# Attention with the values as the stationary operand, output by column, sums by a matrix of ones

## The reference, cut to what matters

```python
q = norm(x) @ Wq.T (+ b_q)           # 16 heads of 16 columns
k, v = ctx @ Wk.T (+ b_k), ctx @ Wv.T (+ b_v)
probs = softmax(q @ k.T / 4)         # over the 77 keys, per head
out = (probs @ v) by heads           # 256 rows x 256 columns
x = x + tanh(g_xattn) * (out @ Wo.T + b_o)
```

## Time and profile before

| | |
|---|---|
| median of 3 runs | 866.01 us |
| profiled execution | 865.35 us, span 863.6 us |
| TensorE busy | 835.3 us (97%) |
| VectorE busy | 539.7 us (62%) |
| ScalarE busy | 427.2 us (49%) |
| attention of layer 0 | about 9 to 145 us |
| attention of layer 1 | about 242 to 382 us |

### The profile page before, as it was taken

How to read it: one execution, slowest core, us unless ns; L and a number is a source line. 1 busy time by engine, 2 the same in 40 slices (tenths; PEclk the granted TensorE clock), 3 DMA queues, 4 the chain that set the end, 5 groups by cost and what they waited for, 6 DMA issues and landing times.

```text
span 863.6 us, 17182 instructions
## 1 busy us (share of the span) xinstructions
PE 835.3 (97%) x5664; PEld 766.5 (89%) x5664; DVE 539.7 (62%) x1132; ACT 427.2 (49%) x938; POOL 276.7 (32%) x329
## 2 busy tenths in 40 slices
PE   8899999999979999999999999999999999999997
PEld 6788988999958989878887999999899999989986
DVE  4777764556687888465446574736456473645558
ACT  3666665777765666532323553616254361615331
POOL 5243414877773452145550001020200102020140
PEclk9999999999999999999999999999999999999999
DMA  5423237877520000201113432314233232413262
GB/s 209 116 69 128 66 117 286 260 219 224 175 77 8 7 6 6 87 17 44 60 44 90 133 90 70 106 41 134 60 97 95 80 89 61 128 39 100 64 194 99
DMA packets 74853, 86.26 MB, mean 100 GB/s; under 512 B 31418, under 2 KB 47484, under 8 KB 74678
## 3 DMA queue, kind: packets, MB, share of 16 engines
q1 hardware_dynamic: 67590, 69.65, 27.0%
q10 hardware_dynamic: 3664, 9.46, 3.1%
q0 software_dynamic: 3552, 6.55, 2.3%
HBM read 63.32 MB, written 23.63 MB: 101 GB/s over the span
## 4 chain that ended last, share of the span: by engine, by line
PE 83%; SPq 5%; DVE 4%; DMA 2%; ACT 2%; issue 2%; POOL 2%; DVEq 0%; ACTq 0%; POOLq 0%
PE score L292 13%; PE score L293 13%; PE score L294 13%; PE bank_p L298 11%; PE bank L603 7%; PE bank_p L299 6%; SPq L371 5%; PE bank_p L594 3%; PE bank L615 3%; PE bank L623 2%; PE bank L544 2%; PE score L583 2%; DMA v_blk<-values 1%; DVE residual L1911 1%; PE bank L957 1%
## 5 line engine op out<-in xcount | busy, mean ns | idle before, releaser
L1257 ACT ACTIVATE silu<-score 128x366 f32<-128x366 f32 (+1 forms) x144 | 72.6, 504 | 274.0 <-PE score L294 274.0
L298 PE MATMUL bank_p<-w_both,hid_hi 128*122 128x512 f32 (+1 forms) x432 | 152.5, 396 | 0.5 <-DVE hid_lo L1653 0.5
L1645 DVE TENSOR_TENSOR prod<-silu,score 128x366 f32<-128x366 f32 (+1 forms) x144 | 82.2, 571 | 110.6 <-ACT silu L1257 109.6
L292 PE MATMUL score<-xe_hi,w_both 128*128 128x366 f32 x448 | 147.4, 329 | 0.0
L293 PE MATMUL score<-xe_lo,w_both 128*128 128x366 f32 x448 | 147.3, 329 | 0.0
L294 PE MATMUL score<-xe_hi,w_both 128*128 128x366 f32 x448 | 147.2, 328 | 0.0
L2165 POOL DMA_INDIRECT slots_out<-yh,home_of x42 | 40.8, 972 | 331.0 <-DVE yh L1802 331.0
L299 PE MATMUL bank_p<-w_both,hid_lo 128*122 128x256 f32 (+1 forms) x432 | 120.8, 280 | 0.0
L298 PEld LDWEIGHTS bank_p<-w_both,hid_hi 128*122 128x122 f32 (+1 forms) x432 | 79.4, 184 | 21.5 <-DVE hid_lo L1653 1.6
L1981 POOL TENSOR_TENSOR w_both<-raw,w_both 128x512 fp32r<-128x512 f32 x62 | 83.4, 1374 | 24.6 <-ACT w_both L1037 17.8
L603 PE MATMUL bank<-v_blk,prob_t 128*128 128x136 f32 x640 | 83.9, 288 | 6.6 <-DMA v_blk<-values 6.2
(11 more groups left out here) (234 smaller groups left out, 1637.5 us busy)
## 6 DMA issues: line engine op xcount, KB each, us to landing
raw<-w_second_d SPq DMA_DIRECT2D x108, 256.0 KB, 2.7
raw<-w_first_d SPq DMA_DIRECT2D x56, 256.0 KB, 3.5
yh<-slot_rows SPq DMA_DIRECT2D x7, 674.6 KB
v_blk<-values SPq DMA_DIRECT2D x256, 5.0 KB, 2.0
slot_rows<-yh ACTq DMA_DIRECT2D x5, 771.0 KB, 3.3
slots_out<-yh ACTq DMA_DIRECT2D x5, 512.0 KB, 4.3
slot_rows<-yh SPq DMA_DIRECT2D x3, 771.0 KB, 5.7
raw<-w_first_d ACTq DMA_DIRECT2D x8, 256.0 KB, 3.8
```

Of the source, the lines that this page charges most:

```text
L292: nc.tensor.matmul(o, a_hi, b_hi, start=start, stop=False)
L298: nc.tensor.matmul(o, a_hi, b.rearrange("p c d -> p (c d)"), start=start, stop=False)
L1257: nc.scalar.activation(silu[0:rows_n, buf, 0:width], src, ACT.Silu).then_inc(silu_done, 1)
L1645: nc.vector.tensor_tensor(prod[0:rows_n, buf, 0:width], silu[0:rows_n, buf, 0:width], up, ALU.mult).then_inc(gu_free, 1)
```

## The change

The values become the stationary operand: for two heads 64 keys x 2 = 128 rows by 32 columns (`v_main`), and for the last 13 keys of the eight heads one full block (`v_rest`). The moving operand is `prob_t`, 256 queries wide. The output has head and dimension on partitions and queries along the row, so it needs no transposition. The sums come from the same matmuls with a matrix of ones. They stand 16 times over (128 partitions x 256), and `normalise_out` takes the reciprocal of all. The probabilities are laid out by head pairs: four transpositions, and for the 13 keys that are left four matmuls with the identity, each 32 columns of the array wide. The value bias goes by one product with Wo into layer 1's output bias. The value loads are 12 DMAs for each batch, into two alternating buffers. The order in the steps is moved accordingly.

```diff
-VW = P + HT
+PAIR = HG * HD                  # 32
+MAIN = P // HG                  # 64 keys
+REST = KV - MAIN                # 13 keys
+PW = KC - P + (-(KC - P)) % 32 + P      # 160
-        prob = [sb(f"prob{u}", [P, PT * P]) for u in range(4)]
-        v_blk = sb("v_blk", [P, KT * PT, VW])
+        prob = [sb(f"prob{u}", [P, ROW_TILES, PW]) for u in range(4)]
+        v_main = sb("v_main", [P, 2, KT * ROW_TILES, PAIR])
+        v_rest = sb("v_rest", [P, 2, KT, P])
...
+            def place_values(g, par):
...
+                if not isinstance(g, int) or g >= 2:
+                    sp.wait_ge(pv_psum, KT * g - KT)
+                for h in range(HG):
+                    for dt in range(KT):
+                        sp.dma_start(v_main[h:P:HG, par, ...], ...)
+                    for hg in range(ROW_TILES):
+                        sp.dma_start(v_rest[hg * 32 + h:hg * 32 + HG * REST:HG, par, :, ...], ...)
...
 prob_transposes:
-                        last = nc.tensor.transpose(bank_p[grp][:, i * P:(i + 1) * P], prob[u][:, j * P:(j + 1) * P], ident[:])
+                        if j < ROW_TILES:
+                            last = nc.tensor.transpose(bank_p[grp][:, i * P:(i + 1) * P], prob[u][:, j, 0:P], ident[:])
+                        else:
+                            for hg in range(ROW_TILES):
+                                last = nc.tensor.matmul(bank_p[grp][hg * PAIR:(hg + 1) * PAIR, i * P:(i + 1) * P],
+                                                        prob[u][:, hg, P:PW], ident[:], start=True, stop=True)
 weighted_values:
+                nc.tensor.matmul(o, v_rest[:, par, dt, :], rest, start=True, stop=False)
+                nc.tensor.matmul(sums, ones_rest[:], rest, start=False, stop=False)
+                for hg in range(ROW_TILES):
+                    nc.tensor.matmul(o[rows, :], v_main[:, par, dt * ROW_TILES + hg, :], prob_t[:, dt * PT + hg, :], start=False, stop=False)
+                for hg in range(ROW_TILES):
+                    last = nc.tensor.matmul(sums[rows, :], ones_main[:], prob_t[:, dt * PT + hg, :], start=False, stop=True)
 project_out:
-                pe.wait_ge(ot_ready, g + 1)
+                pe.wait_ge(ot_ready, KT * g + KT)
 normalise_out (VectorE):
-                nc.vector.reciprocal(recip[:], pv[:, :, P:]).then_inc(recip_done, 1)
+                nc.vector.reciprocal(o_t[:, dt, :], bank[1][:, S:]).then_inc(recip_done, 1)
-                nc.vector.tensor_tensor(o_q..., pv..., recip..., ALU.mult).then_inc(oq_ready, 1)
+                nc.vector.tensor_tensor(o_t[:, dt, :], bank[1][:, 0:S], o_t[:, dt, :], ALU.mult).then_inc(ot_ready, 1)
 TensorE, attention_step, from step 3 on:
   scores 0, 1; prob_transposes(g-1, 2); norm2_t(g-3); project_out(g-2); prob_transposes(g-1, 3);
   norm_t(g+1); wait x_new; weighted_values(g-1, 0); (layer 1: route_logits(g-3) after sub_done 4g+2);
   scores 2, 3; prob_transposes(g, 0); queries(g+1); prob_transposes(g, 1);
   wait ot_ready; weighted_values(g-1, 1)
 VectorE, attention_step, from step 3 on:
   normalise_out(g-2, 1); max_sub 0; norm_stats; add_attention(g-2); max_sub 1; norm2_stats;
   (layer 1: wait s_psum 4g+4; keep_logits); max_sub 2; normalise_out(g-1, 0); max_sub 3; norms
-            def out_transposes(g), def out_t(layer, g)          # gone, with their calls
+            def value_bias():                                   # TensorE, before last_first_down
+                for dt in range(KT):
+                    last = nc.tensor.matmul(bank[0][:, 0:D], bias_cols[:, 1, 2, dt:dt + 1].to_broadcast([P, P]), wa[:, dt, O, :], ...)
 VectorE, attention(1), before half_add is waited for:
+                    nc.vector.scalar_tensor_tensor(out=row[:, 1, :], in0=bank[0][:, 0:D], scalar=tanh_gate[:, 1:2], in1=row[:, 1, :], ...)
 end of attention(1), TensorE:
+   ... shared_gate_up(0, 0); prob_transposes(g, 3); route_logits; project_out(g-1); weighted_values(g, 0); shared_gate_up(0, 1);
+   wait ot_ready; weighted_values(g, 1); shared_gate_up(0, 2); project_out(g); norm2_t(g-1); route_logits; shared_gate_up(0, 3) ...
 end of attention(1), VectorE:
+   normalise_out(g-1, 1); add_attention(g-1); keep_logits; norm2_stats; normalise_out(g, 0); normalise_out(g, 1);
+   shared_hidden(0, 0) ...
```

More of the change, by code:

```diff
@@ L649, in attention_step @@
                     prob_transposes(g - 1, 2)
[L650 to L657, removed]
                 if three:
                     norm2_t(g - 3)
+                if two:
+                    project_out(g - 2, bank[1])
                 if some:
@@ L680, in attention_step @@
                     pe.wait_ge(wa_in, 16)
+                    pe.wait_ge(v_ready, 3)
+                    pe.wait_ge(ones_done, 2)
+                if two:
+                    pe.wait_ge(x_new, g - 1)
                 if some:
-                    pe.wait_ge(oq_ready, KT * g - 1)
+                    weighted_values(g - 1, 1 - par, 0, batches)
+                if layer == 1 and three:
+                    pe.wait_ge(sub_done, 4 * g + 2)
+                    route_logits(g - 3, step_logits)
                 scores(g, par, 2, start)
@@ L691, in attention_step @@
                     queries(g + 1)
[L692 to L696, removed]
                 prob_transposes(g, 1)
@@ L701, in attention_step @@
                     values(0, 2, bank[1])
[L702 to L709, removed]
+                if some:
+                    pe.wait_ge(ot_ready, KT * g - 1)
+                    weighted_values(g - 1, 1 - par, 1, batches)
             def warm_array():
@@ L994, in _ @@
             half_queries(0).then_inc(half_q_psum, 1)
+            pe.wait_ge(wa_in, 32)
+            value_bias()
             last_first_down()
@@ L1094, in probs_t @@
                                          bank_p[grp][:, 0:n * P].rearrange("p (j n) -> p j n", j=n), ACT.Copy).then_inc(pt_ready, 1)
-            def out_t(layer, g):
-                act.wait_ge(ot_psum, g + 1)
-                for dt in range(KT):
-                    last = nc.scalar.activation(o_t[:, dt, :], bank[0][:, dt * S:(dt + 1) * S], ACT.Identity,
-                                                bias=bias_cols[:, layer, 2, dt:dt + 1])
-                last.then_inc(ot_ready, 1)
             def values(layer, i, src):
@@ L1118, in attention_step @@
                     probs_t(g - 1, 2)
-                if two:
-                    out_t(layer, g - 2)
-                if some:
-                    exps(g, 0)
                 if three:
@@ L1141, in attention_step @@
                     exps(g, 0)
-                if not two:
                     exps(g, 1)
@@ L1157, in attention_step @@
                 exps(g, 2)
-                if final_step:
-                    out_t(layer, g - 1)
                 exps(g, 3)
@@ L1532, in attention_step @@
                     add_attention(layer, b - 2, g - 2, bank[1])
+                if not start and not (layer == 1 and n == 0):
+                    max_sub(g, 1, start)
+                if two:
                     norm2_stats(b - 2, g - 2, layer == 0 and n == 2)
+                if layer == 1 and three:
+                    dve.wait_ge(s_psum, 4 * g + 4)
+                    keep_logits(b - 3, step_logits)
                 max_sub(g, 2, start)
-                if final_step:
-                    if layer == 1:
-                        dve.wait_ge(pv_psum, KT * g)
-                        keep_logits(b - 3, bank[1][:, HALVES * VW:])
-                    normalise_out(g - 1, 1)
+                if some:
+                    normalise_out(g - 1, 0)
                 max_sub(g, 3, start)
```

206 lines of the change are left out of this document (103 added, 103 removed).

## The result

The kernel after takes **895.45 us** (median of 4 executions, 892.90 to 898.03), the kernel before beside it 866.71 us (4 executions). The ratio is 1.0336, 95% interval 1.0302 to 1.0369: slower. The forecast was 887 us in a range of 862 to 916. The profiled execution took 896.62 us with a span of 894.8, against 865.35 and 863.6: 31.2 us more, where the forecast's sum had 21.3.

The account below looks back on a forecast made before the run. TensorE was taken to bound both attention loops, with VectorE close behind and becoming the bound. Layer 0 +4.5, before layer 1's loop +1.3 and layer 1 +15.5 make +21.3 on 865.35: 887 us, range 862 to 916.

Parts of the forecast that it names:

- The reciprocal: VectorE, twice a step: 256 numbers per partition instead of 16, 85 ns extra read as per-number cost; 1.77 us, +1.51 each.
- The rival at 2.25 us: VectorE: dearer reciprocal at eight times the plain pace, +0.48 us each, +15, 902 us in all; chance 0.20.
- Column blocks side by side: TensorE: four 32-column matmuls run at once; weighted values of one dt take 1.82 us against 2.35, -0.5.
- Steady steps: Attention loops, bound by VectorE: 15.4 us a step in layer 0 (+1.95), 17.4 in layer 1 (+2.7).
- Layer 1 before its loop: `value_bias` adds 4 passes (0.86 us) on TensorE and the product on VectorE 0.45: +1.3 us.
- the walk: Step-by-step timing of both layers: layer 0 +4.5 us; layer 1 +1.3 before its loop, then +15.5.
- Start of layer 0: Up to the first `max_sub` of step 3: extra reciprocals fall mostly into waits for values, 55.2 us against 54.0.
- Layer 1 from its first `max_sub` to its last `add_attention`: Layer 1's loop and tail: cold TensorE, 17.4 us steps, some 3 us idle in the tail; within the +15.5 us.
- What the shorter list behind the tail gives back: End of layer 1's attention: one gate-up block less to follow the last projection, 2.75 us.
- Cheap reciprocal: VectorE: 256 numbers take 0.50 us, +0.24 each, and the kernel gets faster, 855 us; chance 0.10.
- serial column blocks: TensorE: column blocks run one after another, steps of 20.7 and 22 us, 965 us in all; chance 0.08.
- The clock: Attention loops: TensorE's gaps lower its clock, one 1.8 us loss in every second step, +12, 899 us; chance 0.10.

Follow-up runs that it names:

- the kernels with 0.25 and 0.95 us: The kernel after with each reciprocal taking only 16, or only 128, of the 256 columns of sums: 871.22 us and 876.11 us.

## Why the prediction was right, and where its sum was short

- **The reciprocal** (1.77 us forecast): 1.75. The reading of its 85 ns as a cost for each number was right, and 128 numbers confirmed it. The rival at 2.25 us took eight times the plain pace for it. The Trainium skill, VectorE: DVE Perf Modes, section "Walkthrough: the 8-slice pipeline in each mode", names a repeat count of 8 and no time; the trace shows 6.2 ns for each number, six times the 1.03 of a plain operation.
- **Column blocks side by side:** right. But weighted values took 2.06 us instead of 1.82, and a unit's transpositions 0.94 instead of some 0.85. So TensorE's own step didn't get 0.25 us shorter: with 16-column reciprocals, where TensorE is busy throughout, it is 13.7 and 14.7 us, not 13.2 and 14.5, and in the kernel after TensorE was busy 94% of a layer 0 step, not 85%. This was off the path.
- **Steady steps** (15.4 and 17.4): 15.2 and 17.4, with VectorE's wait in layer 0 0.41 instead of 0.2. From step 3 on layer 0 took 87.2 us to its last `add_attention` (87.8 forecast).
- **Layer 1 before its loop** (+1.3): +1.3. Steps 3 and 7 of layer 1 began within 0.7 us of the walk, shifted by layer 0's loss.

The time lay inside the range, but the sum missed a third of the loss, 9.9 of 31.2 us. Three terms were off by 10.5 us together (0.6 came back in layer 0's steps):

- **Start of layer 0, +4.3.** Step 3 began at 59.5, not 55.2. The step that failed: "Not at the start: all 12 must land" was followed up for batch 1 only. For batch 0 the 12 loads took 9.8 us of queue, at 0.7 to 0.9 each, where the 8 of before took 5.57. The weighted values began at 31.95 and, behind that wait, ran at 1.2 GHz. Of the 4.3 us, 0.5 stood before step 0 (15.82, against 15.31 before), 1.5 went with the clock (43.7 against 42.2 us with the same instructions), and 1.3 with the loads (40.8 without 8 of them); 0.9 is left open.
- **Layer 1 from its first `max_sub` to its last `add_attention`, +4.4.** 0.7 of it had come by the start of step 7, the rest is the tail. The idle of 3 us was forecast and was 2.93. But the gate-up block behind it ran partly at 1.2 GHz and took 403.24 - 399.11 = 4.13 us instead of 2.8. The other 2.4 us stay open, since the forecast doesn't take the tail apart. It says that gate-up blocks hide the projection of g-1; VectorE waited 4.99 us for that projection (until 389.53), and 2.60 us for the last weighted values, which stand behind the second block. Its own numbers also don't close: 391 - 373.35 - 2.75 is 14.9, and the sum has 15.5.
- **What the shorter list behind the tail gives back, +1.8:** 0.9 us from the last `add_attention` to the end, not 2.75.

By the profiled executions, to their last `add_attention` each: layer 0 +8.18 (4.5), before layer 1's loop +1.27 (1.3), layer 1 +22.66 less 0.91 behind it (15.5). That is 31.2.

**The rivals.** Cheap reciprocal and serial column blocks are out by the groups. The clock was no part of the steps, but it was a part of the start and of the tail. And the cheap reciprocal of 0.50 us, had it been real, would have given between 871 and 876 us (the kernels with 0.25 and 0.95 us) and not 855: TensorE's step is longer than forecast, and with such steps the 12 value loads a batch stall again.

## What to carry to other kernels

- A layout that replicates a value (here a sum over 16 columns of its head) multiplies the work of every operation on it. Price the dearest of these per number, by two sizes in the trace: 16 numbers at 257 ns hid a slope of 6.2 ns.
- An engine's slack is the size of change that is free. Here some 1.3 us a step in the new order: going from 16 to 128 numbers cost 5 us, from 128 to 256 another 19. But a wait that follows the engine's own work through another engine isn't slack: in the old order 1.26 us of wait a step outlasted 3.5 us of added work.
- A wait taken from a tail is a gain only if no other stands behind it and the clock doesn't fall. Two edits that brought the last projection forward, the first by 4 us, moved the end by less than these runs can tell.

## What the runs showed of the hardware that was not expected

- An issue of a 256 KB load on ScalarE's queue took 0.6 us when SyncE's queue was moving values (kernel after, DMA share 0.46) or nothing, and 1.2 to 1.4 us when SyncE's queue had six large transfers under way (DMA share 1.00). ScalarE's in-order list then came 3.8 us later, counted from the start of the step, and TensorE waited 5. A queue that gets done sooner can so cost more than it saved.
- 56 us of added VectorE work cost 67 us. In steps of some 19 to 23 us, with TensorE waiting up to 3.1 us at a time, the mean granted clock was 0.88 to 0.90; in the kernel after, idle 1 to 2 us a step, and in the kernel before with the wide reciprocal, idle 2.6 to 2.9, it stayed at 1.00.
- The instructions and one wait don't settle the clock. The same start of layer 0 took 43.7 us at a clock of 0.96 and 42.2 at 1.00, the same start of layer 1 26.7 us at 0.81 and 22.9 at 1.00. Before, 2.73 us of wait at 41.39 were followed by weighted values of 2.56 us, the full pace, and 0.84 us at 257.90 by 4.39 us. A difference of 4 us between two profiled executions can be the clock alone.
